# A sorted mixture of linear layers on one core: the first eight batch numbers from one max operation, other tables read eight at a time

## The reference

```python
# x: [128 batches, 128 rows, 512] fp32; ids: [128] int32 in 0..30
# W: [32, 512, 512] fp32; b: [32, 512] fp32
def reference(x, ids, W, b):
    return x + einsum('bti,bio->bto', x, W[ids]) + b[ids][:, None, :]
```

## Time and profile before

| | before |
|---|---|
| median of 3 runs | 361.41 us (361.26 to 361.68) |
| the profiled execution, whole | 361.15 us |
| span in its profile | 359.3 us |
| PE busy | 354.5 us, 99% of the span |
| POOL, DVE, ACT busy | 268.3, 172.3, 146.8 us |
| TensorE clock granted | 1.00 in every stretch |

### The profile page before, as it was taken

One profiled execution on the slowest core, in us unless ns is written; L12 is line 12 of the kernel. 1 busy time (PEld: TensorE's weight loads), 2 busy tenths in 40 slices (PEclk: granted clock), 3 DMA queues, 4 the chain that ended last, 5 costly groups with the idle time before them and its releaser, 6 DMA issues.

```text
span 359.3 us, 6835 instructions
## 1 busy us (share of the span) xinstructions
PE 354.5 (99%) x1554; PEld 289.7 (81%) x1554; DVE 172.3 (48%) x278; ACT 146.8 (41%) x262; POOL 268.3 (75%) x147
## 2 busy tenths in 40 slices
PE   8999999999999999999999999999999999999996
PEld 3788888888888888888888888888888888888884
DVE  6564454544544544454454454455445445445442
ACT  4563354434433443443443344344344344334420
POOL 3687999998648698799964999799979799934000
PEclk9999999999999999999999999999999999999999
DMA  5999999999887998989997899899998999855532
GB/s 198 327 402 377 383 361 299 332 375 332 336 300 244 368 318 290 301 301 384 329 323 258 287 377 328 273 338 369 332 326 292 368 346 314 317 203 189 188 117 89
DMA packets 43381, 109.51 MB, mean 305 GB/s; under 512 B 4817, under 2 KB 4818, under 8 KB 38610
## 3 DMA queue, kind: packets, MB, share of 16 engines
q1 hardware_dynamic: 37730, 70.01, 53.9%
q0 software_dynamic: 5328, 38.28, 31.4%
q10 hardware_dynamic: 288, 0.79, 0.7%
HBM read 75.50 MB, written 33.55 MB: 304 GB/s over the span
## 4 chain that ended last, share of the span: by engine, by line
PE 98%; DMA 1%; DVE 0%; issue 0%; ACT 0%; SPq 0%
PE pA L429 96%; PE pA L383 1%; DMA xs<-xt 1%; DVE os L376 0%; ACT xh L292 0%; DVE tbc L336 0%; SPq L149 0%; PE pA L400 0%; DVE fill L315 0%; PE pS L393 0%; PE pS L392 0%; SPq L150 0%; SPq L154 0%
## 5 line engine op out<-in xcount | busy, mean ns | idle before, releaser
L376 DVE TENSOR_TENSOR os<-pA,bb 128x512 f32<-128x512 f32 x128 | 88.5, 691 | 170.6 <-PE pA L429 169.7
L292 ACT ACTIVATE xh<-xs 128x512 fp32r<-128x512 f32 x127 | 80.4, 633 | 195.6 <-PE pA L429 125.5
L265 POOL TENSOR_TENSOR wl<-wr,wh 128x2048 fp32r<-128x2048 f32 x30 | 138.7, 4625 | 2.5
L429 PE MATMUL pA<-wh,xh 128*128 x508 | 136.1, 390 | 0.4 <-ACT xh L292 0.4
L429 PE MATMUL pA<-wl,xh 128*128 x508 | 135.8, 390 | 0.0
L429 PE MATMUL pA<-wh,xl 128*128 x508 | 135.8, 390 | 0.0
L429 PEld LDWEIGHTS pA<-wh,xh 128*128 128x128 f32 x508 | 95.3, 188 | 20.3 <-issue 0.8
L429 PEld LDWEIGHTS pA<-wh,xl 128*128 128x128 f32 x508 | 95.4, 188 | 19.9 <-issue 0.3
L429 PEld LDWEIGHTS pA<-wl,xh 128*128 128x128 f32 x508 | 95.4, 188 | 19.8
L341 DVE TENSOR_TENSOR xl<-pT,xh 128x512 fp32r<-128x512 f32 x127 | 86.6, 682 | 10.8 <-ACT pT L295 10.8
L261 POOL TENSOR_SCALAR wh<-wr 128x2048 fp32r<-128x2048 f32 x30 | 57.6, 1921 | 36.3 <-PE pA L429 34.4
(11 more groups left out here) (50 smaller groups left out, 19.7 us busy)
## 6 DMA issues: line engine op xcount, KB each, us to landing
xs<-xt SPq DMA_DIRECT2D x128, 256.0 KB, 5.4
out<-os SPq DMA_DIRECT2D x128, 256.0 KB, 5.0
wr<-w POOLq DMA_DIRECT2D x29, 1024.0 KB, 7.3
bb<-bias POOLq DMA_DIRECT2D x7, 1024.0 KB, 9.6
wr<-w SPq DMA_DIRECT2D x2, 512.0 KB, 5.8
wr<-w SPq DMA_DIRECT2D x1, 1024.0 KB, 9.0
wr<-w ACTq DMA_DIRECT2D x1, 512.0 KB, 3.8
bb<-bias SPq DMA_DIRECT2D x2, 256.0 KB, 7.5
```

Of the source, the lines that this page charges most:

```text
L265: eng.tensor_tensor(wl[:, at], wr[:, c % NR, :], wh[:, at].bitcast(f32), ALU.subtract).then_inc(s_wp if c == 2 else s_w, 1)
L292: eng.activation(xh[:, i % NH, :, :], xs[:, i % NX, :, :], ACT.Copy).then_inc(s_xh, 1)
L376: eng.tensor_tensor(os[:, i % NO, :], pA[i % NA][:, :], bb[:, bass.ds(at, D)], ALU.add)._wait_ge(s_mm, i + 2).then_inc(s_fin, 1)
L429: mm = eng.matmul(pA[i % NA][:, :], xp[:, i % NH, k, :], wp[:, bass.ds(at + k * D, D)], start=(n == 0), stop=(n == 3 * KT - 1))
```

## The change

DVE's key becomes 4095 - 128 * id - i in fp32, from a second, falling iota `rev` that POOL writes first. One `max` operation gives the eight largest keys in falling order, that is the places 0 to 7 in the order of the classes; a key modulo 128 is 127 - i. SP reads two of them at once, issues x of place 0 and, with no wait for s_tab, x of place 1; the other six are read behind the first half of W[1]. The wait for s_tab moves behind the bias row 1 load, ahead of SP's main loop. `table` reads eight entries at a time, but for PE's, which keeps four. On PE the test is turned around, since the key falls with the class: the special path of batch 0 is now in the Else branch.

```diff
-        key = sb("key", [1, 128], i32)
-        low1 = sb("low1", [1, 1], i32)
+        rev = sb("rev", [1, 128], f32)
+        key = sb("key", [1, 128], f32)
+        top = sb("top", [1, 8], i32)
...
-        def table(eng, name, src, n, lo, hi, ahead=4):
+        def table(eng, name, src, n, lo, hi, ahead=8):
...
-            first = eng.alloc_register("first")
+            first = [eng.alloc_register(f"first{i}") for i in range(8)]
+
+            def sorted_first(i):
+                return (B - 1) - eng.snap(first[i], min_val=0, max_val=C * B - 1) % B
+
             eng.wait_ge(s_t0, 1)
-            eng.load(first, low1[0:1, 0:1])
-            x_load(eng, 0, bass.ds(eng.snap(first, min_val=0, max_val=C * B - 1) % B, 1))
+            eng.load(first[:2], top[0:1, 0:2])
+            x_load(eng, 0, bass.ds(sorted_first(0), 1))
             eng.dma_start(raw(0, 3, KT), W[0, :, 3 * D:]).then_inc(s_w0[2], 16)
-            eng.wait_ge(s_tab, 1)
             ahead = table(eng, "la", tbc, B, 0, B - 1)
             behind = table(eng, "st", tbc, B, 0, B - 1)
-            ahead(0)
 
             def load(i):
-                b = ahead(i)
+                b = sorted_first(i) if i < 8 else ahead(i)
...
             load(1)
             w1_load(0)
+            eng.load(first[2:], top[0:1, 2:])
             load(2)
             load(3)
...
             load(5)
             bias_load(eng, 1, 2, s_b0[1])
+            eng.wait_ge(s_tab, 1)
             for i in range(B):
...
         @block.gpsimd
         def _(eng):
+            eng.iota(rev[:, :], [[-1, 128]], base=C * B - 1, channel_multiplier=0,
+                     allow_small_or_imprecise_dtypes=True).then_inc(s_io, 1)
             eng.iota(iot[:, :], [[1, 128]], base=0, channel_multiplier=0,
...
-            link(eng.scalar_tensor_tensor(out=key[:, :], in0=idr[:, :], scalar=float(B), in1=iot[0:1, :],
+            link(eng.scalar_tensor_tensor(out=key[:, :], in0=idr[:, :], scalar=-float(B), in1=rev[:, :],
                                           op0=ALU.mult, op1=ALU.add))
-            eng.tensor_reduce(low1[:, :], key[:, :], AX.X, ALU.min).then_inc(s_t0, 1)
+            eng.max(top[:, :], key[:, :]).then_inc(s_t0, 1)
...
-            eng.wait_ge(s_io, 4)
+            eng.wait_ge(s_io, 5)
...
-            eng.load(lowest, low1[0:1, 0:1])
+            eng.load(lowest, top[0:1, 0:1])
...
-            row = table(eng, "wo", tbc[1:2, :], B, 1, C)
+            row = table(eng, "wo", tbc[1:2, :], B, 1, C, ahead=4)
...
-            with eng.If_lt(lowest, B):
+            with eng.If_lt(lowest, (C - 1) * B):
+                eng.sem_inc(s_raw, 1)
+                one = eng.alloc_register("one")
+                eng.wait_ge(s_tab, 1)
+                eng.load(one, tbc[1:2, 0:1])
+                batch(0, eng.snap(one, min_val=1, max_val=C), early)
+            with eng.Else():
                 eng.wait_ge(s_x[0], 16)
                 for k in range(RAW):
...
-            with eng.Else():
-                eng.sem_inc(s_raw, 1)
-                one = eng.alloc_register("one")
-                eng.wait_ge(s_tab, 1)
-                eng.load(one, tbc[1:2, 0:1])
-                batch(0, eng.snap(one, min_val=1, max_val=C), early)
```

## The result

| | before | after |
|---|---|---|
| median (21 runs each) | 361.28 us (361.01 to 361.99) | 361.83 us (361.55 to 363.81) |
| the profiled execution, whole | 361.15 us | 361.55 us |
| span in its profile | 359.3 us | 359.8 us |

The ratio is 1.0018, with a 95% interval of 1.0011 to 1.0026: the change makes the kernel 0.18% slower, some 0.55 to 0.65 us. Forecast was 0.47 us faster, and the median lies outside the range. The two profiled executions differ by 0.40 us, their spans by 0.44.

What follows compares the result with a forecast made beforehand. PE's matmuls were taken to bound the kernel, leaving only pauses and the start to win. Gains 0.05 + 0.18 + 0.20 + 0.14 less 0.10 gave 0.47 us: 361.41 to 360.94 us, range 360.5 to 361.55.

Steps and rivals of the forecast that it cites:

- What bounds the kernel, and the pauses: PE's 1524 matmuls of line 429 bound it, 346.12 us; pauses stand at batch 1's start, batch 2 and place 9.
- Any delay of this load goes straight to the end: Start: PE runs without a hole from x of place 0 to 9.41; loss 0.10 us, between -0.07 and 0.33.
- The queue has room: SP's queue, 6.5 to 8.0 us: only 76 GB/s, so x of place 1, issued about 4.4, lands near 7.5.
- Two registers at no price: SP's load before x of place 0: two registers cost nothing more, as loads of four are no longer than of one.
- Arithmetic, 0.10: SP's one or two added register operations before x of place 0: loss 0 to 0.25 us, taken as 0.10.
- `max`, 0: DVE's `max` in place of the minimum, on x of place 0's path: -0.07 to +0.08 us, taken as 0.
- The branch, 0.18: PE's sequencer after batch 0: the jump moves to the entry, hidden by warm-up; gain 0.18 us, between 0 and 0.18.
- x of place 1, 0.05: Start of batch 1: x issued some two microseconds earlier, but PE's sequencer was busy itself; gain only 0.05 us.
- Batch 2 (0.20): Start of batch 2: x of place 2 issued at about 5.9 instead of 7.4 closes PE's pause; gain 0.20 us.
- class 2 (0.14): Place 9: earlier bias loads move POOL's release from 31.95 to about 30, closing PE's pause; gain 0.14 us.
- The slower one (a jump that misses its code): PE's entry: the jump into the Else body must fetch its target, time 362.7 us at a 2.66 us fetch; chance 0.05.
- The rival of a wait replaced by something else: Jump keeps its cost, register work costs 0.33, class 2 stays; within 0.2%, 361.2 to 361.5 us; chance 0.22.

Runs made afterwards that it cites:

- f1_branch: The kernel before with only the two paths of batch 0 exchanged and the test turned round; ratio 1.0007.
- e2_early: The kernel before with x of place 1 issued right behind the last quarter of W[0], its batch number a constant; ratio 1.0008.
- f6_hold2: The changed kernel with the load of six registers and a wait for the table put ahead of x of place 1; ratio 1.0003.
- f3_actw: The changed kernel with the last quarter of W[0] issued by ACT as its third transfer, at 1.6 us; ratio 1.0028.
- h1_ring: The kernel before with x of place 1 issued by ACT in ACT's queue, its batch number a constant; ratio 1.0007.
- f2_hole: f1_branch plus second key and max in DVE's idle time, eight registers read behind W[0]'s last quarter, table wait kept before x of place 1; ratio 1.0013.
- g1_hole2: f2_hole without its extra semaphore: the second key and the max count on the minimum's semaphore; ratio 1.0004.
- g4_gap: g1_hole2 without the wait for the table, so x of place 1 goes 1.37 us behind the last quarter of W[0]; ratio 1.0007.
- h5_delay: The kernel before with only the changed kernel's register work on the path of x of place 0; ratio 1.0022.

## Why the prediction was wrong, point by point

- **What bounds the kernel, and the pauses.** Held. The long piece was to shrink to about 345.8; it is 345.75.
- **"Any delay of this load goes straight to the end": the wrong load.** This is the step that failed. The account of costs knew x of place 0 alone. It does arrive 0.23 later, and PE starts on it at 6.43 in place of 6.20, inside the bounds given (-0.07 to 0.33). The last quarter of W[0], issued right behind it and delayed with it, was priced at nothing. Yet its chain (POOL 0.46, ACT 0.63, DVE 0.68, then PE's sequencer) ended 8.90 before, and PE wanted it at 8.95. All the slack in it was the 0.14 us by which DVE was still busy with another slice when ACT was done. The prediction took ACT's 8.08 for the time x of place 1 could be served, and did not follow the same row to PE. The timelines of POOL, DVE and PE in the kernel before, where the first of DVE's two is the quarter's wl and PE's row has the last two products of batch 0:

```profile
6.95 0.46 POOL L229 TENSOR_TENSOR wr<-wr,ident 128x128 f32<-128x128 f32 x1 [0.62 <-DMA wr<-w]
...
8.22 1.28 DVE L350 TENSOR_TENSOR wl<-wr,wh 128x512 fp32r<-128x512 f32 x2
...
8.95 0.62 PE L447 MATMUL pA<-wl,xh 128*128 128x512 f32 x2
```

- **"The queue has room": the second half of the same error.** 76 GB/s between 6.5 and 8.0 describes the hole behind the quarter, not the time at which the quarter is on its way. x of place 1 was to land near 7.5; it landed at 8.62, 3.65 after its issue, and made the quarter 0.4 to 0.7 us late (3.81 against 3.08 to 3.40). Together with the issue, 0.35 later, that is the 1.07 from 6.89 to 7.96.
- **Two registers at no price.** 0.19 us (0.663 against 0.470). That four cost 0.30 was in the earlier trace rows, and was read as "the count does not matter"; it matters in another way. The six cost 1.281 in place of 0.4, and ate the whole advance of x of place 2.
- **Arithmetic, 0.10.** 0.14. `max`, 0: 0.009.
- **The branch, 0.18, and x of place 1, 0.05.** Held as a pair: 0.24 us between the same points in before (1.02) and after (0.78). Neither showed a gain alone: in f1_branch batch 1 began 0.26 us after xh of place 1 was over, in before 0.27, and in e2_early the way from the last wl to batch 1 was 1.01.
- **Batch 2 (0.20) and class 2 (0.14).** The pauses went, and the long piece shrank by the sum forecast, but for another reason. x of place 2 was issued no earlier, and the release of class 2 did not move (31.95). PE came 0.7 to 0.8 us later and so no longer had to wait. It is part of the loss given back, not a gain; in f6_hold2, where batch 1 starts at 10.03, the pause at batch 2 is back, larger (13.23 in place of 12.92). W[2] waits for batch 0 to be over, and so moved with it (10.61 for 10.18), which the prediction had at 9.7.
- **The rivals.** The slower one (a jump that misses its code) did not happen: the branch at 5.2 took 0.230. By the Trainium skill, Runtime: NRT & Kernel Launch, Instruction fetch mechanics, a fetch was to be expected only outside the current pages; no row shows whether this target lay outside them, so the trace bears it out neither way. The rival of a wait replaced by something else had two of its three conditions come true, the register work (0.35 us at the issue) and class 2 where it was, yet at 361.2 to 361.5 it was too fast as well. The mechanism that did make it slower, a transfer issued later and delayed by what is issued behind it, was not among them. Two of the prediction's own signs of being wrong did appear: x of place 0 issued later than 3.7 (3.72), and PE's first product on x after 6.3 (6.43).

The loss, put together: 1.07 for the quarter, less 0.14 of slack, less 0.24 for the hand-over, plus 0.12 of slightly longer steps on the way, is the 0.81 at batch 1; less 0.37 of pauses is 0.44 of span. Beside f6_hold2, which has the later issue and the hand-over but no crowding and starts batch 1 at 10.03, 0.06 of the 0.81 are those two together and 0.75 the crowding; both sums rest on single executions.

## What to carry to other kernels

Before a transfer is moved forward, list every transfer that will be on its way at that time, and follow each to the last engine that waits for it; the one with the least slack sets what the move costs, and it need not be the one ahead of it in the same queue. If an engine waits 0.4 us for an operand, find out from its sequencer how much of that is its own register work. Then look at what the engines on that chain do when the operand comes: here 0.28 us of landing were worth nothing, since POOL's add waited out an operation of DVE. And a pause that closes downstream of a new delay is the delay being absorbed, so count it once.

## What the runs showed of the hardware that was not expected

- Register loads on SP took 0.47 us for one value, 0.66 for two, 0.30 for four, 1.28 for six and 0.53 to 0.72 for eight. Four or eight at once are the cheap sizes; two and six are not between them. The six were read from the third entry of their tile on, all others from its start or a multiple of four; no run separates the number from the place.
- A 256 KB load whose successor follows within 0.5 to 1.4 us landed 3.53 to 3.87 us after its issue in six executions; with a gap of 2 us, or only 2 KB behind it, 3.08 to 3.40 in nine. In the one execution with the successor in another queue it was 3.57.
- POOL's add of the identity (128x128, 0.45 us alone) and DVE's operations on the same stretch for the most part did not run side by side: the one that began second took longer, POOL's up to 0.80 us and DVE's up to 0.98 in place of 0.69.
- In the profiled execution of f3_actw PE sat idle 1.06 us before batch 0. Its first four products took 2.79 us to the next one, in the changed kernel, after 0.59 us idle, 1.42. From 11.42 to 13.5 the products came one every 0.43 us, from 14.55 on one every 0.23, though the clock column of the profile reads 1.00 throughout; 512 columns in 0.43 us is 1.2 GHz, the lower of its two levels. PE's timeline in f3_actw:

```profile
7.41 3.78 PE L450 MATMUL pA<-wr,xs 128*128 128x512 f32 x4 [1.06 <-DMA xs<-xt]
...
11.84 0.63 PE L460 MATMUL pA<-wh,xh 128*128 128x512 f32 x1
12.27 0.63 PE L460 MATMUL pA<-wh,xl 128*128 128x512 f32 x1
```

- The time outside the span goes with the kernel: 1.75 to 1.89 us in most (one execution of before had 2.07), 1.87 to 2.13 in h1_ring, 2.09 to 2.21 in f2_hole, g1_hole2, g4_gap and h5_delay. The spans of the profiled executions alone would have ranked f2_hole first.
